# c and q of a recommender kernel: z's tiles as the stationary operand, both weights moved past them together

## The reference

```python
for Wk, bk in zip([W0, W1, W2], [b0, b1, b2]):
    z = jnp.einsum('bid,bjd->bdij', base, curr)
    curr = jnp.einsum('bdij,ijh->bhd', z, Wk) + bk[None, :, None]
    logit.append(curr)
pooled = jnp.sum(jnp.concatenate(logit, axis=1), axis=-1)
out = pooled @ lin_w + lin_b
```

## Time and profile before

| | us |
|---|---|
| median of 3 runs | 178.92 |
| lowest, highest | 178.66, 179.82 |
| the profiled execution | 178.86 |
| its span on the core | 177.0 |

### The profile page before, as it was taken

One profiled execution on the slowest core, in us unless ns is written; L12 is line 12 of the kernel. 1 busy time (PEld: TensorE's weight loads), 2 busy tenths in 40 slices (PEclk: granted clock), 3 DMA queues, 4 the chain that ended last, 5 costly groups with the idle time before them and its releaser, 6 DMA issues.

```text
span 177.0 us, 2496 instructions
## 1 busy us (share of the span) xinstructions
PE 171.7 (97%) x798; PEld 118.3 (67%) x798; DVE 151.7 (86%) x141; ACT 73.3 (41%) x80; POOL 10.1 (6%) x20
## 2 busy tenths in 40 slices
PE   6799999999999999999999999999999999999995
PEld 1462766777777777777777777777777777777762
DVE  0998765699999999999999999999999999995022
ACT  4564710244642464246423644264425642440020
POOL 3231605000000000000000000000000000000000
PEclk9999999999999999999999999999999999999999
DMA  5999655999886777867785778487857850000000
GB/s 177 345 385 342 192 145 168 420 412 407 258 243 245 211 208 224 293 169 236 226 329 136 231 236 313 154 236 220 272 185 226 228 177 0 0 0 0 4 0 0
DMA packets 12524, 36.53 MB, mean 206 GB/s; under 512 B 2532, under 2 KB 4036, under 8 KB 12516
## 3 DMA queue, kind: packets, MB, share of 16 engines
q1 hardware_dynamic: 11376, 35.84, 62.4%
q10 hardware_dynamic: 1140, 0.59, 1.4%
HBM read 35.35 MB, written 1.07 MB: 206 GB/s over the span
## 4 chain that ended last, share of the span: by engine, by line
PE 90%; DMA 4%; SPq 3%; DVE 1%; issue 0%; ACT 0%; DVEq 0%
PE c_ps L502 43%; PE q_ps L502 42%; DMA w_post<-w1x 4%; PE q_ps L604 2%; SPq L198 1%; SPq L202 1%; PE q_ps L511 1%; SPq L194 1%; PE c_ps L667 1%; PE c_ps L671 1%; SPq L187 0%; DVE acc L362 0%; DVE w_post L290 0%; PE c_ps L549 0%; PE q_ps L549 0%
## 5 line engine op out<-in xcount | busy, mean ns | idle before, releaser
L373 ACT ACTIVATE z_high<-xb_z 126x1024 fp32r<-126x1024 f32 x56 | 59.2, 1060 | 77.8 <-DVE xb_z L269 76.1
L276 DVE TENSOR_TENSOR z_low<-xb_z,z_high 126x1024 fp32r<-126x1024 f32 x56 | 68.0, 1217 | 0.9 <-ACT z_high L373 0.9
L269 DVE TENSOR_TENSOR xb_z<-x_a,xb_z 126x1024 f32<-126x1024 f32 x49 | 59.6, 1217 | 3.3 <-DMA xb_z<-xw 3.2
L502 PE MATMUL c_ps<-z_high,wc_high 126*101 126x512 f32 x112 | 35.1, 395 | 0.4 <-ACT z_high L373 0.4
L502 PE MATMUL c_ps<-z_low,wc_high 126*101 126x512 f32 x112 | 35.1, 395 | 0.0
L502 PE MATMUL c_ps<-z_high,wc_low 126*101 126x512 f32 x112 | 35.0, 394 | 0.0
L502 PE MATMUL q_ps<-z_high,wq_high 126*101 126x512 f32 x108 | 33.8, 394 | 0.0
L502 PE MATMUL q_ps<-z_low,wq_high 126*101 126x512 f32 x108 | 33.7, 393 | 0.0
L502 PE MATMUL q_ps<-z_high,wq_low 126*101 126x512 f32 x108 | 33.6, 392 | 0.0
L502 PEld LDWEIGHTS c_ps<-z_high,wc_low 126*101 126x101 f32 x112 | 18.5, 165 | 7.5
L502 PEld LDWEIGHTS c_ps<-z_high,wc_high 126*101 126x101 f32 x112 | 18.4, 165 | 7.6 <-issue 0.5
(11 more groups left out here) (58 smaller groups left out, 59.9 us busy)
## 6 DMA issues: line engine op xcount, KB each, us to landing
xb_z<-xw SPq DMA_DIRECT2D x49, 512.0 KB, 4.4
x_a<-xa SPq DMA_DIRECT2D x7, 512.0 KB, 5.2
w_d<-w2h SPq DMA_DIRECT2D x4, 404.0 KB, 5.7
w_post<-w1x SPq DMA_DIRECT2D x3, 512.0 KB, 7.1
pair_sb<-w_pairs SPq DMA_DIRECT2D x3, 202.0 KB, 8.1
x_a<-xa SPq DMA_DIRECT2D x2, 256.0 KB, 3.2
w_post<-w1x SPq DMA_DIRECT2D x2, 252.5 KB, 8.0
d_dram<-w_d SPq DMA_DIRECT2D x2, 189.4 KB, 2.9
```

The lines of the kernel that those rows point to most:

```text
L269: nc.vector.tensor_tensor(xb_z[0:K, c, :], x_a[0:K, u % 2, :], x_b, ALU.mult).then_inc(z_done, 1)
L276: nc.vector.tensor_tensor(z_low[0:K, m % SLOTS, :], xb_z[0:K, c, :], z_high[0:K, m % SLOTS, :].bitcast(fp32), ALU.subtract).then_inc(low_d ...
L373: nc.scalar.activation(z_high[0:K, m % SLOTS, :], xb_z[0:K, m % C, :], ACT.Copy).then_inc(high_done, 1)
L502: end = nc.tensor.matmul(ps[0:J, h * B:(h + 1) * B], w[0:K, c * J:(c + 1) * J], z[0:K, slot, h * B:(h + 1) * B], start=(c == 0 and first), ...
```

## The change

From unit 1 on the operands change places. A tile of 128 columns of z (PT) is stationary (126 × 128) and a slice of 202 columns of the weights moves: c's and q's weights lie side by side in one tile `weights` (c high, q high, c low, q low, 101 columns each), so slot 0 to 1 is the high pair and slot 2 to 3 the low pair. A chunk is 24 matmuls (`tile_pass`): 8 tiles for z_high with the high pair, 8 for z_high with the low pair, 8 for z_low with the high pair. The psum tile of a unit is 128 partitions × 8 tiles × 256 columns (202 used), c in the first 101 and q in the next. Samples are now on the partitions and the 101 indices in the columns.

ACT copies c after the unit (128 × 808 elements, ahead of rounding chunk 2 of the next unit), DVE multiplies q by it (after forming chunk 3 of the next unit) with no add; ACT then sums the product along the columns with four activations with `accum_out`, each over the two values of d (202 elements), into a column of `stats`. ACT's loop is written out. Unit 0 keeps the old form; its product goes straight to acc. Ahead of the last chunk PE sums acc with 8 fp32 matmuls and adds the sums of units 1 to 6 with 6 fp32 matmuls against an identity (`ident`, a new input, 64 KB, loaded behind unit 1's xb). The last chunk runs in two halves of 4 tiles; each half is copied by ACT, multiplied and reduced by DVE, and added by one matmul. The pieces that prepare the weights do the same work with other strides.

```diff
 NCH = U * C
 SLOTS = 2 * C
 BODY = 2 * C
-PRODUCT_AT = 16
-C1_AT = 2 * C - 1
+PRODUCT_AT = C + 3
+C1_AT = C + 2
...
 SMALL = LW_AT + OR
-
-
-def build(nc, xa, xw, w0_pairs, w1x, w2h, pick, small, out):
+PT = 128
+TILES = N // PT
+BTS = B // PT
+TP = 256
+STATS = BTS * U
+TPB = B // TP
+
+
+def build(nc, xa, xw, w0_pairs, w1x, w2h, pick, small, ident, out):
     fp32, f32r = mybir.dt.float32, mybir.dt.float32r
...
-        wc_low = sb("wc_low", [128, C * J], f32r)
-        wq_high = sb("wq_high", [128, C * J], f32r)
-        wq_low = sb("wq_low", [128, C * J], f32r)
+        weights = sb("weights", [128, C, 4 * J], f32r)
+        ident_sb = sb("ident_sb", [PT, PT])
...
 
-        c1_sb = [w1_post[0:J, i * N:(i + 1) * N] for i in range(2)]
-        prod = w1_post[0:J, 2 * N:3 * N]
-
-        c1_ps = [ctx.enter_context(nc.psum_tensor(f"c1_ps{i}", [128, N], fp32)) for i in range(2)]
-        q_ps = [ctx.enter_context(nc.psum_tensor(f"q_ps{i}", [128, N], fp32)) for i in range(2)]
+        c1_sb = w1_post[0:J, 0:N]
+        c_sb = [w1_post[:, i * N:i * N + TILES * J].rearrange("p (t j) -> p t j", j=J) for i in range(2)]
+        prod = w1_post[:, 2 * N:2 * N + TILES * J].rearrange("p (t j) -> p t j", j=J)
+        prod_pairs = w1_post[:, 2 * N:2 * N + TILES * J].rearrange("p (d t j) -> p t d j", t=BTS, j=J)
+
+        ps = [ctx.enter_context(nc.psum_tensor(f"ps{i}", [128, 2 * N], fp32)) for i in range(2)]
+        c1_ps = [ps[i][:, 0:N] for i in range(2)]
+        q_ps = [ps[i][:, N:2 * N] for i in range(2)]
+        tiles_ps = [ps[i].ap().rearrange("p (t n) -> p t n", n=TP) for i in range(2)]
 
         sel_ps = (c1_ps[0],) + (c1_ps[1], q_ps[0]) * (SELECTED // 2 + 1)
         warm_ps = q_ps[1][:, 0:B]
...
+            sp.dma_start(ident_sb[:, :], ident).then_inc(ident_loaded, 16)
             with sp.Fori(0, U // 2 - 1) as it:
...
+            def first_product():
+
+                dve.wait_ge(z_slots_free, SLOTS + C)
+                dve.wait_ge(c1_copied, 1)
+                nc.vector.tensor_tensor(acc[:, :], q_ps[0][0:J, :], c1_sb, ALU.mult).then_inc(q_psum_free, 1)
+
             def product(it, u):
 
                 dve.wait_ge(z_slots_free, it * BODY + (SLOTS + C * (u + 1)))
                 dve.wait_ge(c1_copied, it * 2 + (u + 1))
-                dve.wait_ge(acc_done, it * 2 + (u + 1))
-                nc.vector.tensor_tensor(prod, q_ps[u % 2][0:J, :], c1_sb[u % 2], ALU.mult).then_inc(q_psum_free, 1)
-                dve.wait_ge(q_psum_free, it * 2 + (u + 3))
-                nc.vector.tensor_tensor(acc[:, :], acc[:, :], prod, ALU.add).then_inc(acc_done, 1)
-
-            def last_product(cols):
-
-                nc.vector.tensor_tensor(prod[:, cols], q_ps[1][0:J, cols], c1_sb[1][:, cols],
-                                        ALU.mult).then_inc(last_done, 1)
+                dve.wait_ge(summed, it * 2 + u)
+                nc.vector.tensor_tensor(prod, tiles_ps[u % 2][:, :, J:2 * J], c_sb[u % 2], ALU.mult
+                                        ).then_inc(q_psum_free, 1)
+
+            def last_product(h):
+
+                dve.wait_ge(half_done, h + 1)
+                dve.wait_ge(half_copied, h + 1)
+                nc.vector.tensor_tensor(prod[:, half_tiles(h), :], tiles_ps[1][:, half_tiles(h), J:2 * J],
+                                        c_sb[1][:, half_tiles(h), :], ALU.mult).then_inc(half_multiplied, 1)
+                dve.wait_ge(half_multiplied, h + 1)
+                first = BTS * (U - 2 + h)
+                nc.vector.tensor_reduce(stats[:, first:first + BTS], prod[:, half_tiles(h), :],
+                                        mybir.AxisListType.X, ALU.add).then_inc(half_summed, 1)
 
             def form_first(h):
                 cols = slice(h * B, (h + 1) * B)
...
-                    if m >= PRODUCT_AT and (m - PRODUCT_AT) % C == 0:
+                    if m == PRODUCT_AT:
+                        first_product()
+                    elif (m - PRODUCT_AT) % C == 0:
                         product(it, (m - PRODUCT_AT) // C)
                     if m > C:
                         split(it, m - 1)
...
             split(0, NCH - 1)
-            product(0, U - 2)
-            dve.wait_ge(acc_done, U)
-            nc.vector.tensor_tensor(acc[:, 0:B], acc[:, 0:B], acc[:, B:N], ALU.add).then_inc(acc_done, 1)
-            dve.wait_ge(c1_copied, U)
-            dve.wait_ge(last_q_done, 1)
-            last_product(slice(0, B))
-            dve.wait_ge(last_done, 1)
-            dve.wait_ge(acc_done, U + 1)
-            nc.vector.tensor_tensor(acc[:, 0:B], acc[:, 0:B], prod[:, 0:B], ALU.add).then_inc(acc_done, 1)
-            dve.wait_ge(last_q_done, 2)
-            last_product(slice(B, B + B // 2))
-            last_product(slice(B + B // 2, N))
+            dve.wait_ge(summed, U - 1)
+            last_product(0)
+            last_product(1)
 
         @block.scalar
         def _(act):
...
-            def copy_c1(it, u):
-
-                act.wait_ge(c1_done, it * 2 + (u + 1))
-                if u >= 1:
-                    act.wait_ge(q_psum_free, it * 2 + (u + 1))
-                nc.scalar.activation(c1_sb[u % 2], c1_ps[u % 2][0:J, :], ACT.Copy).then_inc(c1_copied, 1)
-                act.wait_ge(c1_copied, it * 2 + (u + 1))
-                act.sem_inc(c1_psum_free, 1)
+            def copy_first_c():
+
+                act.wait_ge(c1_done, 1)
+                nc.scalar.activation(c1_sb, c1_ps[0][0:J, :], ACT.Copy).then_inc(c1_copied, 1)
+
+            def copy_c(u):
+
+                act.wait_ge(z_slots_free, SLOTS + C * (u + 1))
+                nc.scalar.activation(c_sb[u % 2], tiles_ps[u % 2][:, :, 0:J], ACT.Copy).then_inc(c1_copied, 1)
+
+            def copy_last_c(h):
+
+                act.wait_ge(half_done, h + 1)
+                nc.scalar.activation(c_sb[1][:, half_tiles(h), :], tiles_ps[1][:, half_tiles(h), 0:J], ACT.Copy
+                                     ).then_inc(half_copied, 1)
+
+            def sum_product(u):
+
+                act.wait_ge(q_psum_free, 2 + (u + 1))
+                for t in range(BTS):
+                    k = BTS * (u - 1) + t
+                    nc.scalar.activation(prod_pairs[:, t], prod_pairs[:, t], ACT.Copy,
+                                         accum_out=stats[:, k:k + 1]).then_inc(summed_parts, 1)
+                act.wait_ge(summed_parts, BTS * u)
+                act.sem_inc(summed, 1)
 
             def copy_d(g):
...
+                    act.sem_inc(summed, 1)
                 if m == C1_AT:
-                    copy_c1(0, 0)
+                    copy_first_c()
                 round_high(0, m)
-            with act.Fori(0, NCH // BODY - 1) as it:
-                for m in range(BODY, 2 * BODY):
-                    if (m - C1_AT) % C == 0:
-                        copy_c1(it, (m - C1_AT) // C)
-                    round_high(it, m)
-            copy_c1(0, U - 1)
+            for m in range(BODY, NCH):
+                if (m - C1_AT) % C == 0:
+                    copy_c((m - C1_AT) // C)
+                round_high(0, m)
+                if (m - PRODUCT_AT) % C == 0:
+                    sum_product((m - PRODUCT_AT) // C)
+            copy_last_c(0)
+            copy_last_c(1)
             act.wait_ge(total_done, 1)
             nc.scalar.activation(out_sb[:, :], out_ps, ACT.Identity, bias=const_sb[:, 0:1]).then_inc(out_ready, 1)
 
...
                                     ALU.subtract).then_inc(last_ready, 1)
 
         @block.tensor
         def _(pe):
-            def chunk_pass(ps, w, z, m, first, last):
-
-                c, slot = m % C, m % SLOTS
+            def chunk_pass(bank, s, z, m, first, last):
+
                 for h in range(2):
-                    end = nc.tensor.matmul(ps[0:J, h * B:(h + 1) * B], w[0:K, c * J:(c + 1) * J],
-                                           z[0:K, slot, h * B:(h + 1) * B],
-                                           start=(c == 0 and first), stop=(c == C - 1 and last))
+                    end = nc.tensor.matmul(bank[0:J, h * B:(h + 1) * B], weights[0:K, m, s * J:(s + 1) * J],
+                                           z[0:K, m, h * B:(h + 1) * B],
+                                           start=(m == 0 and first), stop=(m == C - 1 and last))
                 return end
 
-            def last_q(m, cols):
-
-                c, slot = m % C, m % SLOTS
-                for k, (w, z) in enumerate(((wq_high, z_high), (wq_high, z_low), (wq_low, z_high))):
-                    last = nc.tensor.matmul(q_ps[1][0:J, cols], w[0:K, c * J:(c + 1) * J], z[0:K, slot, cols],
-                                            start=False, stop=(c == C - 1 and k == 2))
-                return last
-
-            def c1_chunk(it, m):
+            def tile_pass(z, w, m, t, first=False):
+
                 u, c = divmod(m, C)
+                return nc.tensor.matmul(tiles_ps[u % 2][:, t, 0:2 * J], z[0:K, m % SLOTS, t * PT:(t + 1) * PT],
```

(108 more changed lines are left out.)

56 lines of the change are left out of this document (24 added, 32 removed).

## The result

| | before | after |
|---|---|---|
| median, us | 179.06 (20 runs) | 177.99 (20 runs) |
| lowest to highest | 178.44 to 180.46 | 176.99 to 179.25 |
| ratio after to before, with 95% interval | | 0.994, 0.9922 to 0.9959 |
| the profiled execution | 178.86 | 178.15 |
| its span | 177.0 | 176.4 |

The change makes the kernel 1.1 us faster, 0.6%, where 3.5 us were forecast. The direction and the mechanism came out as forecast, the size did not, and the direction hung on less than the prediction's rows could resolve (see the part on why it was wrong).

A forecast was written before the change was run, and what follows sets the result against it. PE's matmul stream was taken as the bound, then its weight loads after the change: 36.65 + 129.36 + 3.05 + 4.47 = 173.5 us of span, plus 1.86 around it, 175.4 us; range 170 to 195.

The forecast's parts named there:

- part 1: PE's stream of units 1 to 7: load-bound pairs at 110 ns, 129.4 us against 136.1, with the granted clock full.
- the pairs of the earlier trace: 128-column f32r loads behind an idle array in the trace before the change, 0.11 us apart; basis for 110 ns.
- the chain of the earlier trace: Loads of 101 columns with 64-column matmuls between, in the trace before the change: 0.09 us each, 0.114 scaled to 128.
- The formula: Whole time as 46.03 + 1176 p, p the pitch of a load and matmul pair; break-even at p = 113 ns.
- The opening: First unit and its preparation, up to PE's first matmul of unit 1: 36.65 us of span.
- Part 2: DVE and ACT beside PE's stream: costed at nothing, DVE needing 16.8 us a unit against PE's 18.5.
- Part 3: Sums over acc and stats on PE's path before the last chunk: 14 fp32 matmuls, +3.05 us.
- part 4: Tail after PE's last matmul slot: 4.47 us against 4.28 before, including a reduction of about 0.58.
- The handover rival: On PE's pairs, 16 ns on top of the load: 126 ns, 194.2 us; chance 0.26 between 114 and 127 ns.
- The narrow stream: PE's 202 moved f32r columns: 91 to 101 ns estimated; rival at fp32's rate 339 ns, 444.7 us, chance 0.10.
- Load and stream: Rival on PE's pairs: load and moving time add up, 110 + 91 = 201 ns, 282 us; chance 0.04.
- The load that is cheap at exactly 128 columns: Rival on PE's weight loads: stream or DVE then sets the pace, 164 to 165 us; chance 0.06.

The follow-up runs named there:

- Experiment 2: Kernel after, with stationary tiles 32 to 128 columns wide in chunks 1 to 6 of units 2 to 6, 202 columns moved: 168.32 us in one run.
- experiment 6: Kernel after, z_low's pass reading bf16: 170.61 us; both correction passes in bf16: 163.23 us; both, with DVE folding the fp32 sums' inputs: 162.1 us.
- experiment 3: Kernel after, with 32, 64, 100, 160, 180 and 202 moved columns in chunks 1 to 6 of units 2 to 6, loads 128: 231.97 us in one run.
- experiment 4: Kernel after, with 180, 202, 160, 202, 130 and 202 moved columns in chunks 1 to 6 of units 2 to 6: 178.9 us in one run.

## Why the prediction was wrong

Term by term, against the profiled execution:

| term | predicted, us | measured, us |
|---|---|---|
| up to unit 1 | 36.65 | 37.44 |
| 1,176 pairs | 129.36 | 128.62 + 24 × 0.1117 = 131.30 |
| fp32 sums | 3.05 | 1.84 + 1.31 = 3.15 |
| tail | 4.47 | 176.4 − (169.21 + 2.68) = 4.51 |
| around the span | 1.86 | 1.75 |
| sum | 175.4 | 178.15 |

- **The step that failed is the pitch in part 1**, a size and not a mechanism: 110 ns, taken where the pairs of the earlier trace rows stand, against 111.7. It is worth 1.9 us of the 2.6 by which 175.4 misses the median, and over half of the forecast gain of 3.5. Experiment 2 gives what the pitch is made of: 128 columns at 0.833 ns are 106.7, and 5.0 more.
- **The rows could not give the pitch to 2 ns.** A distance read from times printed to 0.01 us is open by several ns: read to the nanosecond, the trace has 108 and 109 for the pairs of the earlier trace rows and 88 and 90 for the chain of the earlier trace rows, where the line of experiment 2 gives 111.7 and 89.2. The running chain of 101 columns lies on the line, the pairs behind an idle array 3 ns under it; why these are closer was not tested. Nor was the chain scaled by 128/101 the better number: it also scales the fixed part and gives 0.114, 180.1 us by the formula, 2.1 us too slow. The prediction's own rows allowed a better sum, 0.81 × 128 for the columns and 90 − 0.81 × 101 for the fixed part, 112 ns, though open by several ns; it was not made.
- **The formula held**: 46.03 + 1176 p gives 177.4 us with the measured pitch, 0.6 from the median.
- **That the direction was right is in part luck.** Break-even was p = 113, the measured pitch is 111.7, and the rows left 106 to 114 open. The point 110 and the chain's 114 stood on either side of break-even.
- **The opening** was read from one profile. It spreads over 2 us, and the 0.8 us by which the term was missed can't be put down to the change.
- **Part 2 was right**: the product and the copy come 3 and 2 chunks behind their unit, DVE waits 1.7 us a unit, PE in the stream for nobody. Its floor of 16.8 us a unit was met in experiment 6.
- **The clock came out right, for a reason that does not hold.** It stayed up, as forecast, but part 1 said "since the array is never left idle". In experiment 3 PE and its loader are recorded as busy all the time and the granted clock still falls to 0.50.
- **Part 3 and part 4 were right** to 0.1 us: 3.15 for 3.05, the tail 4.51 for 4.47, the reduction 0.58 for 0.58.
- **The rivals.** The handover rival was right in kind (there is a charge on top of the load) and wrong in size: 5 ns on top of 106.7, not 16 on top of 110. The charge of 16 ns that I read out of the 512-column pitch does not add to a load. The narrow stream costs 94 ns, inside the 91 to 101 estimated. Load and stream do not add up: 111.7 is less than 106.7 and 94 together, so the rule on row groups in the Trainium skill, "TensorE: Matmul & The Clock Gate", section on packing small matmuls, does not hold here.
- **The load that is cheap at exactly 128 columns exists, but not for f32r.** Recorded loads of bf16 take 126 ns for 101 columns and 98 for 128: more columns, less time. F32r's 128 stay on the line of the others. This is what the Trainium skill has on that page under "Weight-path perf modes", with the one addition that f32r counts as FP32 there. The prediction gave this case 0.06 for f32r, rightly low, and did not ask what the change would be worth with operands that qualify.
- **The chances.** "Same" had 0.14 and "faster by over 1%" 0.52, though the 1% band (111.5 to 114.5 ns) took 2.5 ns of the likeliest range of 106 to 114, and what came is inside that band. The time lay inside the stated range of 170 to 195.

## What to carry to other kernels

When the narrower operand becomes the moving one, put down both prices of a matmul, columns loaded and columns moved, and take the larger for each pair; here 128 loaded f32r columns (111.7 ns) covered 202 moved ones (94 ns) and a change that moves 21% fewer columns gave 0.6%. Then ask which operand type makes the larger of the two cheap: correction passes in bf16 gave 8% more in this form and 1% in the old one. If hundreds of equal pairs carry the sum, ask how well the rows give the pitch: here 1 ns was 1.18 us, and single distances printed to 0.01 us could not tell a gain of 3.5 us from a loss of 1. Take it over a long run of equal instructions where there is one, price load and fixed part apart, and where there is none let the range and the chances say so.

## What the hardware showed that was not expected

- A narrow stream behind full loads lets the granted clock fall with PE recorded as busy throughout: 1.00 to 0.50 after chunks with 32 and 64 moved columns to 128 loaded ones, and 231.97 us for less work (experiment 3). Once down it stayed at 0.50 through 100, 160 and 180 moved columns and came back with 202. With 130 to 202 columns from a full clock it stayed at 1.0 (experiment 4), and in the kernel after as well.
- At the lower clock the 24 pairs of a chunk of 100 moved columns take 5.14 us (64.06 to 69.20), 214 ns each and twice 106.7 to within 1 ns; the 5 ns on top at the full clock are not seen there.
- Pairs that their load does not bound start 94 ns apart with 202 moved columns in f32r and 91 in bf16, and 231.6 and about 226 apart with 512: between the two widths 0.44 ns a column, not the 0.42 of the earlier trace rows.
